# Inverses of sums in slices, two transfers and a sum moved, and one product earlier at a hand-over between two stages

## The chip, the cores and the metric

One core of one Trainium2 chip. The metric is the device time of one execution in microseconds (us), the median of several runs.

## The reference

Four sequences of 2,048 tokens with 256 channels go through pre-norm attention with 16 heads of 16 channels and then a gated feed-forward step with a shift by one token:

```
...
    logits = jnp.einsum('bhnd,bhmd->bhnm', q, k) * INV_SCALE
    attn = jax.nn.softmax(logits, axis=-1)
    h = jnp.einsum('bhnm,bhmd->bhnd', attn, v)
    concat_h = h.transpose(0, 2, 1, 3).reshape(B, N, C)
    return concat_h @ Wo.T + bo
...
        xr = mu_r * x + (1.0 - mu_r) * x_prev
        xk = mu_k * x + (1.0 - mu_k) * x_prev
        r = jax.nn.sigmoid(jnp.einsum('btc,dc->btd', xr, W_r))
        k = jnp.einsum('btc,dc->btd', xk, W_k)
        k_act = jnp.square(jax.nn.relu(k))
        out = r * jnp.einsum('btc,dc->btd', k_act, W_v)
...
x = x + attention(layernorm(x))
x = x + ffn(layernorm(x))
```

The last two lines are shortened from the reference's own.

## The kernel before

Every engine has its program written out by hand, in two stages that run into each other, and waits by semaphores. A `Steps` object is a semaphore with named steps per block: `done` counts one on, `wait(engine, block, name)` waits for it.

**The first stage** (`stage_attend`) projects q, k and v for 16 blocks of 512 tokens and then does attention in 64 rounds (`ITS`; `it` is the round, `pit` the round whose maxima are taken). A round is one group of four heads by 512 queries against 2,048 keys. It has two periods of eight steps each (`SPAN`; 128 `PERIODS`). The softmax needs each query's maximum score first. So the main loop runs two things beside each other, three periods (`LEAD`) apart: TensorE computes score tiles only to take their maxima (`peaks`, L1193), VectorE reduces each (`maxima`, L999, and L994 with ScalarE's copies), 14 packs of two reductions a period. Behind that TensorE computes the scores again, transposed (`scores`, L1137), ScalarE takes their exponentials (L922), and TensorE multiplies these with v (`times_v`, L1234). v has a column of ones, so the product holds the sum of the exponentials too. Three PSUM banks serve the maxima in turn. ScalarE copies a round's output (`keep_output`, L936) and SyncE stores it to `sums` (L706).

**What comes in ahead.** `MixInputs` prepares the second stage while the first runs. `load_constants` and `load_sums` fetch the weights and the sums of exponentials of three sequences. `invert` is VectorE's reciprocal of them (L287), 256 elements in each of 128 partitions for a sequence. `store_inverse` writes it to memory and `load_heads` reads it back spread over channels, with the numerators. GpSimd multiplies both (`heads`, L317) and adds the output bias to x (`add_to_x`, L326). VectorE's `spread_bias` and `shares_left` (L333, L352) are small preparations. All of it is placed by round on SyncE (`if it == ITS - 6`) and by period on VectorE (`first_pack(PERIODS - 6)`).

**The hand-over.** In the last three periods no maxima are left, so VectorE and the maxima's banks (5 to 7) are free. `early(k)`, k from 0 to 23, puts work of the second stage between TensorE's steps: products with Wo (`project`, L443) for blocks 0 to 3 and the turns of blocks 0 and 1 (`turn`, L453). VectorE takes each result as it comes: `residual` (L363, and statistics L367), `first_normalised` (L422), then `first_turned`, which copies a turned block out of PSUM (L431) and multiplies by the shares mu_k and mu_r (L435), and `shift` (L413), which adds the previous token's part. `free_ahead` makes TensorE wait for the bank that it writes next. The sums of x and bias of blocks 2 and 3 need x of these blocks. SyncE loads it only when the residual of two blocks before has read the buffer (`load_x`).

**The second stage** (`stage_mix`) goes over the 16 blocks in pairs. For each: product with Wk (`key`, L1649), with Wr (`receptance`, L1623), square of the rectified k (ScalarE), product with Wv (`value`, L1623), the gate times that (`gated`, L1583), and in between the residual, statistics, turn and shift of later blocks. `receptance(0)` writes banks 4 and 5, and bank 4 is where attention's output accumulates. So it waits for `s_oe`, ScalarE's copy of the last round.

The line numbers here and in the rows are those of the kernel before.

Of the kernel before, what the change touches and what calls it, by code (L numbers as in the profile page):

```python
# [21 lines left out]
P = 128  # L22
B, N, C, H = 4, 2048, 256, 16
D = C // H
KH = C // P
# [176 lines left out]
class MixInputs:  # L202
# [9 lines left out]

    EARLY, FREE = 2, 3

    def __init__(self, ctx, nc, x, sums_d, rden_d, bv, woT, bo, wrT, wkT, wvT, mu_r, mu_k):
# [68 lines left out]

    def invert(self, dve, seq):
        dve.wait_ge(self.s_den[seq], DMA)
        dve.reciprocal(self.inv[:, seq, :], self.den[:, seq, :]).then_inc(self.s_inv, 1)  # L287

    def store_inverse(self, sp, seq):
        sp.wait_ge(self.s_inv, seq + 1)  # L290
        sp.dma_start(self.rden_d[seq].rearrange("h (a w) -> (h a) w", w=self.W), self.inv[:, seq, :]
                     ).then_inc(self.s_rden[seq], DMA)
# [181 lines left out]
def stage_attend(ctx, nc, psum, x, wqT, wkT, wvT, bq, bk, q_d, k_d, kd_d, v_d, sums_d, inputs, ahead):  # L474
# [28 lines left out]
    FILLS_AHEAD = 4  # L503
    TURN_AT = 7
    FIRST_LEAD = QB + 2
    LEADS = [4] + [5] * 8 + [4]
# [164 lines left out]
    def sync(sp):  # L671
# [41 lines left out]
        def body(it):  # L713
            sp.wait_ge(s_st, unit(it * CH, 0) + 1)
            sp.wait_ge(s_vc, (it // QB) * CH + CH)
            now = range(pieces(it - 1), pieces(it))
            for n in now:
                inputs.load_k(sp, n)
            for n in now:
                inputs.load_kd(sp, n)  # L720
            for n in now:
                inputs.load_v(sp, n)
            if it + QRING - 1 < ITS:
                inputs.load_q(sp, it + QRING - 1)
            if it + 1 < ITS:
                rows(it + 1)
            sp.wait_ge(s_k, K_INC * pieces(it))
            sp.wait_ge(s_kd, K_INC * pieces(it))
            sp.wait_ge(s_v, V_INC * pieces(it))
            sp.wait_ge(s_q, Q_INC * min(it + QRING, ITS))  # L730
            out(it)
# [35 lines left out]
        for it in range(ITS):  # L767
            if it == ITS - 6:
                ahead.load_constants(sp)
                for seq in range(B - 1):  # L770
                    ahead.load_sums(sp, seq)
# [7 lines left out]
            if it == ITS - 3:  # L779
                for n in range(2, 4):  # L780
                    ahead.load_heads(sp, n)
            if it == ITS - 1:
                ahead.load_x(sp, 2)
                for seq in range(1, B - 1):
                    ahead.store_inverse(sp, seq)
                ahead.load_x(sp, 3)
                sp.wait_ge(ahead.s_rden[1], DMA)
                for n in range(4, 6):
                    ahead.load_heads(sp, n)
                for n in range(4, 6):  # L790
                    ahead.load_x(sp, n)
            body(it)

    def gpsimd(pool):
# [70 lines left out]
        for n in range(4):  # L865
            if n >= 2:
                ahead.heads(pool, n)
            ahead.add_to_x(pool, n)

# [103 lines left out]
    def vector(dve):  # L973
# [132 lines left out]
        for n in range(FULL * LEAD, PACKS):  # L1106
            if n == first_pack(PERIODS - 6):
                ahead.spread_bias(dve)
                ahead.shares_left(dve)
                ahead.invert(dve, 0)  # L1110
            maxima(n)
        of_block(ITS - 1)
        ahead.add_bias(dve, psum[:, ahead.bank_ahead(2), 0:C])
        for seq in range(1, B - 1):
            ahead.invert(dve, seq)
        for blk in range(2):
# [13 lines left out]

    def tensor(te):
        def scores(it, c, pair):
# [266 lines left out]
        for n in range(SPAN * (PERIODS - LEAD), STEPS):  # L1399
            last_fills(n, 1, n + 1, 0)  # L1400
            early(n - SPAN * (PERIODS - LEAD))
            last_fills(n + 1, 0, n + 1, 1)
            times_v(n)

# [3 lines left out]
def stage_mix(ctx, nc, psum, inputs, out):  # L1408
# [165 lines left out]
    def vector(dve):  # L1574
# [24 lines left out]
        for blk in range(0, BLOCKS, 2):  # L1599
# [3 lines left out]
            if blk == 0:  # L1603
                inputs.invert(dve, B - 1)
            if blk + 2 < BLOCKS:
# [10 lines left out]
            if blk + 4 < BLOCKS:  # L1616
                inputs.means(dve, blk // 2 + 2)
                inputs.newton(dve, blk // 2 + 2)

    def tensor(te):  # L1620
# [17 lines left out]

        def key(blk):
            vb.wait(te, blk, f"mk{KH - 1}")  # L1640
            if blk == 0:
                dx.wait(te, 2 * EARLY - 1, "x11")
            elif blk < LAST - 1:
                vy.wait(te, blk - 1, "gated")
            else:
                at.wait(te, blk, "xT1")
            for h in range(KH):
                for k in range(KH):
                    mm = te.matmul(psum[:, key_at(blk) + h, :], w_sb["k"][:, k, h * P:(h + 1) * P],  # L1649
                                   mixed["mk"][blk % 2][:, k, :], start=(k == 0), stop=(k == KH - 1))  # L1650
            pk.done(mm)

        def receptance(blk):
# [17 lines left out]

        for steps in (pk, pr, pv):
            steps.start(te)
        for blk in range(0, BLOCKS, 2):
            more = blk + 4 < BLOCKS
            key(blk)
            receptance(blk)
            if blk + 1 == LAST:
                key(blk + 1)
            value(blk)  # L1680
            receptance(blk + 1)
            if blk + 1 < LAST:
                key(blk + 1)
                turned(blk + 2)
# [8 lines left out]

    return sync, gpsimd, scalar, vector, tensor


def build(nc, a):
# [7 lines left out]
    with ExitStack() as ctx:  # L1705
# [29 lines left out]
        @block.tensor  # L1735
        def _(te):
            first[4](te)
            last[4](te)
# [23 lines left out]
```

## Time and profile before

| | |
|---|---|
| median of 3 runs | 2800.03 us (2799.42 to 2801.36) |
| the profiled execution | 2800.92 us, of which the span from first to last instruction is 2799.1 |
| busy: TensorE (PE) | 2742.8 us, 98% of the span |
| VectorE (DVE) | 2496.4 us, 89% |
| ScalarE (ACT) | 2492.9 us, 89% |
| GpSimd (POOL) | 372.9 us, 13% |
| chain that ended last | 78% TensorE, 10% SyncE's queue, 5% ScalarE, 3% VectorE |

In the attention loop three engines are near full together. Matmuls overlap in TensorE's pipeline and their ends are modelled, so its 98% does not mean that it could take in nothing more. The time is then read from who waits for whom, stage by stage. Times are in us from the start of the span.

### The profile page before, as it was taken

The page shows a single profiled execution, that of the slowest core. Times are in us where ns is not written, and L with a number is a line of the kernel's source. Part 1 is how long each engine was busy: PE and PEld are TensorE (multiplying, and loading weights), DVE is VectorE, ACT ScalarE, POOL GpSimd, SP SyncE. Part 2 cuts the span into 40 slices and gives each one's busy share as a digit, 9 for nine tenths or more (in the row PEclk, how much of TensorE's full clock was granted, in tenths as well). Part 3 has the DMA queues.
Part 4 walks back from the last instruction along what each step waited for, and adds up shares of the span by engine and source line. Part 5 has one row for each costly group of instructions (what it writes and reads, how often), then busy time and mean ns, then how long its engine had stood idle before and what let it go on. Part 6 is the DMA issues. An engine that isn't in the chain of part 4 may idle for free.

```text
span 2799.1 us, 59961 instructions
## 1 busy us (share of the span) xinstructions
PE 2742.8 (98%) x23628; PEld 924.0 (33%) x23628; DVE 2496.4 (89%) x4797; ACT 2492.9 (89%) x2874; POOL 372.9 (13%) x751
## 2 busy tenths in 40 slices
PE   8999999999999999999999999999999999999999
PEld 4543222222222222222222222222222222224776
DVE  4567999999999999999999999999999999985774
ACT  6767999999999999999999999999999999996555
POOL 6762000000000000000000000000000000113451
PEclk9999999999999999999999999999999999999999
DMA  4642000000000000101010101010100001212431
GB/s 161 206 152 79 22 22 22 22 22 22 22 22 22 20 24 15 29 9 31 11 33 11 33 11 33 11 33 11 31 13 27 17 20 42 58 36 87 157 129 46
DMA packets 135288, 124.34 MB, mean 44 GB/s; under 512 B 49888, under 2 KB 117344, under 8 KB 135008
## 3 DMA queue, kind: packets, MB, share of 16 engines
q1 hardware_dynamic: 135008, 120.52, 14.0%
q8 instruction: 187, 3.06, 0.4%
q14 instruction: 93, 0.76, 0.1%
HBM read 72.75 MB, written 47.19 MB: 43 GB/s over the span
## 4 chain that ended last, share of the span: by engine, by line
PE 78%; SPq 10%; ACT 5%; DVE 3%; issue 2%; DMA 2%; ACTq 0%; DVEq 0%
PE psum L1234 33%; PE psum L1137 17%; PE psum L1193 15%; SPq L153 3%; PE psum L1257 3%; PE psum L1623 2%; SPq L158 2%; PE psum L1152 2%; PE psum L443 2%; SPq L126 2%; SPq L127 2%; DMA a_qs<-q_parts 2%; PE psum L1268 2%; PE psum L1649 2%; ACT m_gate L922 1%
## 5 line engine op out<-in xcount | busy, mean ns | idle before, releaser
L999 DVE TENSOR_REDUCE a_mx<-psum 128x1 f32<-128x512 f32 x3096 | 1948.6, 685 | 121.3 <-PE psum L1193 100.5
L1137 PE MATMUL psum<-a_qs,a_ks 50*128 50x512 f16 x4096 | 793.2, 384 | 11.8 <-ACT m_gate L922 1.2
L922 ACT ACTIVATE m_gate<-psum 128x1024 f32<-128x1024 f32 x684 | 674.5, 1034 | 41.2 <-PE psum L1137 38.3
L922 ACT ACTIVATE p_x<-psum 128x1024 f32<-128x1024 f32 x682 | 672.7, 1034 | 41.6 <-PE psum L1137 39.0
L1193 PE MATMUL psum<-a_ks,a_qs 48*128 48x512 f16 x3596 | 696.2, 383 | 13.7 <-DVE a_mx L999 5.5
L922 ACT ACTIVATE m_y<-psum 128x1024 f32<-128x1024 f32 x682 | 672.7, 1034 | 38.6 <-PE psum L1137 35.8
L1234 PE MATMUL psum<-m_gate,a_vst 128*32 128x256 f32 (+1 forms) x4568 | 414.8, 435 | 1.6 <-ACT m_gate L922 0.9
L1234 PE MATMUL psum<-p_x,a_vst 128*32 128x256 f32 (+1 forms) x4568 | 412.4, 433 | 0.8
L1234 PE MATMUL psum<-m_y,a_vst 128*32 128x256 f32 (+1 forms) x4552 | 411.8, 433 | 0.8
L1137 PEld LDWEIGHTS psum<-a_qs,a_ks 50*128 50x128 f16 x4096 | 199.1, 93 | 610.1 <-ACT m_gate L922 135.2
L994 DVE CUSTOM_DVE_ANT_0 a_copied<-psum,a_copied 128x512 f32<-128x512 f32 x500 | 323.6, 685 | 23.6 <-PE psum L1193 23.6
L1193 PEld LDWEIGHTS psum<-a_ks,a_qs 48*128 48x128 f16 x3596 | 175.0, 93 | 463.6 <-DVE a_mx L999 368.3
L931 ACT ACTIVATE a_copied<-psum 128x1024 f32<-128x1024 f32 x250 | 260.6, 1042 | 0.1
L808 POOL MEMSET a_mx<- 128x8 f32 x64 | 7.2, 112 | 1384.9 <-DVE a_m L978 1384.9
L801 POOL COPY a_vst<-a_vin 128x64 f32<-128x64 f32 x256 | 59.7, 236 | 754.4 <-PE psum L1234 754.4
L1234 PEld LDWEIGHTS psum<-m_gate,a_vst 128*32 128x32 f32 x4568 | 90.5, 108 | 191.5 <-issue 174.7
L1234 PEld LDWEIGHTS psum<-p_x,a_vst 128*32 128x32 f32 x4568 | 90.6, 108 | 189.9 <-issue 175.1
L1234 PEld LDWEIGHTS psum<-m_y,a_vst 128*32 128x32 f32 x4552 | 90.2, 108 | 190.0 <-issue 174.7
L1152 PE MATMUL psum<-a_kd,a_qs 48*128 48x512 f16 x500 | 97.2, 381 | 0.0
L823 POOL TENSOR_TENSOR m_split<-m_whole,m_split 128x512 f16<-128x512 f32 x64 | 73.6, 1156 | 74.1 <-ACT m_split L910 73.7
L908 ACT ACTIVATE m_whole<-psum,p_sb,p_gain 128x512 f32<-128x512 f32 x64 | 49.4, 772 | 28.9 <-PE psum L1257 28.8
L363 DVE TENSOR_TENSOR m_whole<-psum,m_x 128x512 f32<-128x512 f32 x24 | 16.5, 690 | 56.6 <-PE psum L443 56.6
(126 smaller groups left out, 1636.9 us busy)
## 6 DMA issues: line engine op xcount, KB each, us to landing
m_x<-x SPq DMA_DIRECT2D x24, 512.0 KB, 5.8
a_qs<-q_parts SPq DMA_DIRECT2D x384, 32.0 KB, 2.1
sums<-a_o SPq DMA_DIRECT2D x256, 34.0 KB
q_parts<-m_split SPq DMA_DIRECT2D x16, 512.0 KB, 3.2
v_rows<-m_v SPq DMA_DIRECT2D x16, 512.0 KB, 2.7
k_parts<-m_split SPq DMA_DIRECT2D x16, 512.0 KB, 3.9
a_ks<-k_parts SPq DMA_DIRECT2D x64, 128.0 KB
a_vin<-v_rows SPq DMA_DIRECT2D x64, 128.0 KB, 5.5
```

Source lines behind the costliest of these rows:

```text
L153: sp.dma_start(self.qs[row:row + D, it % QRING, :].rearrange("p (u t) -> p u t", u=GP), src[a, par]).then_inc(self.s_q, DMA)
L801: pool.tensor_copy(v_st[:, c, :, 0:D], v_in[:, u % 2, c, :].rearrange("p (g d) -> p g d", g=G)).then_inc(s_vc, 1)
L823: least.done(pool.tensor_tensor(parts[s][:, j, 1, :], full[s][:, j, :], parts[s][:, j, 0, :], ALU.subtract))
L922: ac.activation(p_sb[n % WEIGHTS][:, 2 * pair:2 * pair + 2, :], psum[:, at:at + 2, :], ACT.Exp, scale=SCALE).then_inc(s_exp, 1)
L931: ac.activation(copied[:, :, :], psum[:, at:at + 2, :], ACT.Relu).then_inc(s_exp, 1)
L994: dve.tensor_tensor_reduce(out=copied[:, par, :], in0=psum[:, bank(at), :], in1=copied[:, par, :], scale=1.0, scalar=LEAST, op0=ALU.add, o ...
L999: dve.tensor_reduce(peak, psum[:, bank(at), :], AX.X, ALU.max).then_inc(s_mx, 1)
L1137: mm = te.matmul(psum[:, pair_of_banks(u) + par, :], ks[row:row + MR, (it // QB) % 2, pair, c * P:(c + 1) * P], qs[row:row + MR, it % QRIN ...
L1152: mm = te.matmul(psum[:, pair_of_banks(u) + par, :], qs[row:row + SR, pit % QRING, at:at + P], kd[row:row + SR, (pit // QB) % 2, pair, :], ...
L1193: te.matmul(psum[:, bank(slot(n, par)), :], qs[row:row + SR, pit % QRING, at:at + P], keys, start=True, stop=True).then_inc(s_sp, 1)
L1234: mm = te.matmul(psum[32 * g:32 * g + 32, O, at:at + width], v_st[:, c, g, :], p_sb[n % WEIGHTS][:, g, at:at + width], start=(c == 0), sto ...
L1257: mm = te.matmul(psum[:, j % 2, :], w_sb[n][:, k, h * P:(h + 1) * P], xnT[blk % 2][:, k, :], start=(k == 0), stop=(k == KH - 1))
```

## The change

Four edits:

1. `invert` becomes eight slices of 32 elements (`SLICES`). Those of sequences 0 to 2 (24 slices) are put one in every five packs (`APART`) of the maxima, from sixteen periods before the end on. The copies of `spread_bias` and the `shares_left` go to the starts of the eighteenth and the seventeenth period before the end. Before, both and the inverse of sequence 0 stood in one place six periods before the end, and the inverses of sequences 1 and 2 stood after the last maximum. Sequence 3's inverse, in the second stage, is cut into eight slices in its place. The loads of weights and sums move from round `ITS - 6` to `ITS - 11`.
2. On SyncE the load of x of block 2 goes into the round before last, behind the rows of maxima, and the stores of the inverses of sequences 1 and 2 go to round `ITS - 3`. Both stood at the start of the last round.
3. GpSimd's sum for block 3 waits for VectorE's last share of block 1 (`mr1`).
4. TensorE's product with Wk of block 0 is issued ahead of the last product with v.

```
-    def invert(self, dve, seq):
-        dve.wait_ge(self.s_den[seq], DMA)
-        dve.reciprocal(self.inv[:, seq, :], self.den[:, seq, :]).then_inc(self.s_inv, 1)
+    def invert(self, dve, seq, n):
+
+        if n == 0:
+            dve.wait_ge(self.s_den[seq], DMA)
+        at = bass.ds(n * (self.W // self.SLICES), self.W // self.SLICES)
+        dve.reciprocal(self.inv[:, seq, at], self.den[:, seq, at]).then_inc(self.s_inv, 1)
...
+            if it == ITS - 2:
+                ahead.load_x(sp, 2)
...
-            if it == ITS - 6:
+            if it == ITS - 11:
                 ahead.load_constants(sp)
...
             if it == ITS - 3:
                 for n in range(2, 4):
                     ahead.load_heads(sp, n)
-            if it == ITS - 1:
-                ahead.load_x(sp, 2)
                 for seq in range(1, B - 1):
                     ahead.store_inverse(sp, seq)
+            if it == ITS - 1:
                 ahead.load_x(sp, 3)
...
+            if n == 3:
+                ahead.at.wait(pool, 1, f"mr{KH - 1}")
             ahead.add_to_x(pool, n)
...
-            if n == first_pack(PERIODS - 6):
+            if n == first_pack(PERIODS - 18):
                 ahead.spread_bias(dve)
+            if n == first_pack(PERIODS - 17):
                 ahead.shares_left(dve)
-                ahead.invert(dve, 0)
+            piece, left = divmod(n - first_pack(PERIODS - 16), APART)
+            if left == 0 and 0 <= piece < (B - 1) * ahead.SLICES:
+                ahead.invert(dve, piece // ahead.SLICES, piece % ahead.SLICES)
             maxima(n)
         of_block(ITS - 1)
         ahead.add_bias(dve, psum[:, ahead.bank_ahead(2), 0:C])
-        for seq in range(1, B - 1):
-            ahead.invert(dve, seq)
...
+            if n == STEPS - 1:
+                beside_last(te)
             times_v(n)
...
-                inputs.invert(dve, B - 1)
+                for n in range(inputs.SLICES):
+                    inputs.invert(dve, B - 1, n)
...
+    def first_key(te):
+
+        pk.start(te)
+        key(te, 0)
```

`beside_last` is `first_key` of the second stage. `key` moved out of that stage's TensorE program unchanged, which no longer calls it for block 0.

On VectorE, at the sixth period before the end (`a_mx` the maxima, `m_inv` the inverses, `m_den` the sums), the kernel before has:

```order
L994 ISA a_mx 128x1
L333 COPY m_bvs<-m_bv 128x128 x2
L352 TENSOR_SCALAR m_restmk<-m_mk 128x2
L352 TENSOR_SCALAR m_restmr<-m_mr 128x2
L287 RECIPROCAL m_inv<-m_den 128x256
L999 TENSOR_REDUCE a_mx<-psum 128x1
```

Nothing stands between the maxima there now. Ten periods earlier the changed kernel has this, where the one before has reductions alone:

```order
L291 RECIPROCAL m_inv<-m_den 128x32
L1007 TENSOR_REDUCE a_mx<-psum 128x1
L986 TENSOR_REDUCE a_m<-a_mx 128x16
L1007 TENSOR_REDUCE a_mx<-psum 128x1 x5
L1002 ISA a_copied,a_mx<-psum,a_copied 128x512
L1002 ISA a_mx 128x1
L1002 ISA a_copied,a_mx<-psum,a_copied 128x512
L1002 ISA a_mx 128x1
L1007 TENSOR_REDUCE a_mx<-psum 128x1 x2
L291 RECIPROCAL m_inv<-m_den 128x32
L1007 TENSOR_REDUCE a_mx<-psum 128x1 x10
L291 RECIPROCAL m_inv<-m_den 128x32
```

Ten reductions, five packs, lie from slice to slice.

On SyncE's queue over the last rounds (`a_mrows` the rows of maxima, `sums` a round's store) the kernel before has:

```order
L699 DMA a_qs<-a_mrows 1x8x128 x4
L706 DMA sums<-a_o 17x512 x4
L699 DMA a_qs<-a_mrows 1x8x128 x4
L706 DMA sums<-a_o 17x512 x4
L308 DMA m_x<-x 128x4x256
L291 DMA inverse_denominators<-m_inv 128x256 x2
L308 DMA m_x<-x 128x4x256
L301 DMA m_num<-sums 128x1x512
```

and the changed one:

```order
L295 DMA inverse_denominators<-m_inv 128x256 x2
L704 DMA a_qs<-a_mrows 1x8x128 x4
L711 DMA sums<-a_o 17x512 x4
L704 DMA a_qs<-a_mrows 1x8x128 x4
L312 DMA m_x<-x 128x4x256
L711 DMA sums<-a_o 17x512 x4
L312 DMA m_x<-x 128x4x256
L305 DMA m_num<-sums 128x1x512
```

The two stores of inverses moved ahead of two rounds, and the first load of x ahead of one store of sums.

On TensorE, where the first stage ends (L1234 is v, L1649 Wk, L1623 Wr and Wv), before:

```order
L1137 MATMUL psum<-a_qs,a_ks 128x512 x4
L1234 MATMUL psum<-p_x,a_vst 32x512 x4
L1234 MATMUL psum<-m_gate,a_vst 32x512 x4
L1649 MATMUL psum<-m_split,m_wk 128x512 x4
L1623 MATMUL psum<-m_wr,m_split 128x256 x8
```

and in the changed kernel:

```order
L1146 MATMUL psum<-a_qs,a_ks 128x512 x4
L1243 MATMUL psum<-p_x,a_vst 32x512 x4
L1642 MATMUL psum<-m_split,m_wk 128x512 x4
L1243 MATMUL psum<-m_gate,a_vst 32x512 x4
L1654 MATMUL psum<-m_wr,m_split 128x256 x8
```

The product with Wk stands between the last two with v now, and Wr's follows the last with v directly.

## Rows read from the trace of the kernel before

**Rows 1.** Timeline, SyncE's queue, stores of sums: start, length, engine, line, operation, count.

```profile
1834.14 1.27 SPq L706 DMA_DIRECT2D sums<-a_o  x4
1870.28 1.27 SPq L706 DMA_DIRECT2D sums<-a_o  x4
1906.71 1.28 SPq L706 DMA_DIRECT2D sums<-a_o  x4
...
2377.09 1.28 SPq L706 DMA_DIRECT2D sums<-a_o  x4
...
2416.53 1.27 SPq L706 DMA_DIRECT2D sums<-a_o  x4
```

**Rows 2.** Timeline, VectorE, six periods before the end of the maxima.

```profile
2392.25 0.36 DVE L333 COPY m_bvs<-m_bv 128x128 f32<-128x128 f32 x2
...
2392.59 0.16 DVE L352 TENSOR_SCALAR m_restmr<-m_mr 128x2 f32<-128x2 f32 x1
2392.66 1.75 DVE L287 RECIPROCAL m_inv<-m_den 128x256 f32<-128x256 f32 x1
2394.32 0.63 DVE L999 TENSOR_REDUCE a_mx<-psum 128x1 f32<-128x512 f32 x1
```

**Rows 3.** Windows: length, busy (count) of PE, PEld, DVE, ACT, POOL, granted clock, DMA.

```profile
2395.00:2398.60 3.60, 3.59 (x16) 0.58 (x16) 2.14 (x5) 0.64 (x1) 0.94 (x5) 0.53 0.00 0
...
2548.80:2552.20 3.40, 3.40 (x11) 1.47 (x14) 3.37 (x8) 0.75 (x1) 0.00 (x0) 0.50 0.43 163
```

**Rows 4.** Timeline, VectorE, an ordinary period; brackets hold the wait before a row.

```profile
2306.21 0.69 DVE L994 CUSTOM_DVE_ANT_0 a_copied<-psum,a_copied 128x512 f32<-128x512 f32 x1 [0.36 <-PE psum L1193]
...
2307.44 11.31 DVE L999 TENSOR_REDUCE a_mx<-psum 128x1 f32<-128x512 f32 x18
```

**Rows 5.** Waits over the whole span: us in total, times, longest.

```profile
PEld psum L1193 <- DVE a_mx L999: 368.3, 895, 1.9
```

**Rows 6.** Timeline, TensorE at the hand-over, products with Wo.

```profile
2541.01 1.13 PE L443 MATMUL psum<-m_wo,m_hT 128*128 128x256 f32 x4
...
2543.71 1.13 PE L443 MATMUL psum<-m_wo,m_hT 128*128 128x256 f32 x4
...
2548.80 2.07 PE L443 MATMUL psum<-m_wo,m_hT 128*128 128x256 f32 x4 [2.31 <-DVE m_xT L431]
...
2553.07 1.13 PE L443 MATMUL psum<-m_wo,m_hT 128*128 128x256 f32 x4
```

**Rows 7.** Timeline, VectorE at the hand-over, shares of mu and a residual.

```profile
2537.98 3.45 DVE L435 TENSOR_SCALAR m_split<-m_xT,m_mk 128x512 f32<-128x512 f32 x2
2541.35 3.99 DVE L435 TENSOR_SCALAR m_split<-m_xT,m_mr 128x512 f32<-128x512 f32 x2
...
2549.25 0.88 DVE L435 TENSOR_SCALAR m_split<-m_xT,m_mk 128x512 f32<-128x512 f32 x2
...
2553.69 1.28 DVE L363 TENSOR_TENSOR m_whole<-psum,m_x 128x512 f32<-128x512 f32 x2
```

**Rows 8.** Timelines of GpSimd, SyncE's queue and VectorE at the hand-over.

```profile
2537.36 2.36 POOL L326 TENSOR_TENSOR m_x<-m_x,m_bo 128x1024 f32<-128x1024 f32 x1 [17.01 <-DMA m_x<-x]
...
2542.52 2.54 POOL L326 TENSOR_TENSOR m_x<-m_x,m_bo 128x1024 f32<-128x1024 f32 x1
...
2529.14 0.40 SPq L308 DMA_DIRECT2D m_x<-x  x1
...
2517.72 0.69 DVE L363 TENSOR_TENSOR m_whole<-psum,m_x 128x512 f32<-128x512 f32 x1 [4.64 <-PE psum L443]
```

**Rows 9.** Timelines of TensorE and ScalarE where the first stage ends.

```profile
2568.73 1.07 PE L1234 MATMUL psum<-m_gate,a_vst 128*32 128x512 f32 x8 [0.88 <-ACT m_gate L922]
...
2573.27 1.03 PE L1623 MATMUL psum<-m_wr,m_split 128*128 128x256 f32 x4
...
2569.87 0.58 ACT L936 COPY a_o<-psum 128x512 f32<-128x512 f32 x1 [1.19 <-PE psum L1234]
```

**Rows 10.** Timeline, VectorE, first pair of the second stage.

```profile
2597.96 1.22 DVE L1583 TENSOR_TENSOR m_y<-psum,m_gate 128x1024 f32<-128x1024 f32 x1
```

More of the change, by code:

```diff
@@ L213 @@
     EARLY, FREE = 2, 3
+    SLICES = 8
     def __init__(self, ctx, nc, x, sums_d, rden_d, bv, woT, bo, wrT, wkT, wvT, mu_r, mu_k):
@@ L283, in load_sums @@
                      ).then_inc(self.s_den[seq], DMA)
-    def invert(self, dve, seq):
-        dve.wait_ge(self.s_den[seq], DMA)
-        dve.reciprocal(self.inv[:, seq, :], self.den[:, seq, :]).then_inc(self.s_inv, 1)
+    def invert(self, dve, seq, n):
[3 more added lines that the diff above has]
+        dve.reciprocal(self.inv[:, seq, at], self.den[:, seq, at]).then_inc(self.s_inv, 1)
     def store_inverse(self, sp, seq):
-        sp.wait_ge(self.s_inv, seq + 1)
+        sp.wait_ge(self.s_inv, (seq + 1) * self.SLICES)
         sp.dma_start(self.rden_d[seq].rearrange("h (a w) -> (h a) w", w=self.W), self.inv[:, seq, :]
@@ L504, in stage_attend @@
     TURN_AT = 7
+    APART = 5
     FIRST_LEAD = QB + 2
@@ L1129, in vector, with tensor @@
         ahead.newton(dve, 1)
-    def tensor(te):
+    def tensor(te, beside_last):
         def scores(it, c, pair):
@@ L1618, in vector, with key @@
                 inputs.newton(dve, blk // 2 + 2)
+    def key(te, blk):
+        vb.wait(te, blk, f"mk{KH - 1}")
+        if blk == 0:
+            dx.wait(te, 2 * EARLY - 1, "x11")
+        elif blk < LAST - 1:
+            vy.wait(te, blk - 1, "gated")
+        else:
+            at.wait(te, blk, "xT1")
+        for h in range(KH):
+            for k in range(KH):
+                mm = te.matmul(psum[:, key_at(blk) + h, :], w_sb["k"][:, k, h * P:(h + 1) * P],
+                               mixed["mk"][blk % 2][:, k, :], start=(k == 0), stop=(k == KH - 1))
+        pk.done(mm)
+    def first_key(te):
+        pk.start(te)
+        key(te, 0)
     def tensor(te):
@@ L1637, in turned @@
             inputs.turn(te, blk, [psum[:, turned_at(blk) + h, :] for h in range(KH)])
[L1639 to L1651, printed above, removed]
         def receptance(blk):
@@ L1670, in value @@
                     pv.done(mm)
-        for steps in (pk, pr, pv):
+        for steps in (pr, pv):
             steps.start(te)
@@ L1675, in tensor @@
             more = blk + 4 < BLOCKS
-            key(blk)
+            if blk:
+                key(te, blk)
             receptance(blk)
             if blk + 1 == LAST:
-                key(blk + 1)
+                key(te, blk + 1)
             value(blk)
@@ L1682, in tensor @@
             if blk + 1 < LAST:
-                key(blk + 1)
+                key(te, blk + 1)
                 turned(blk + 2)
@@ L1692, in tensor @@
                 proj(blk + 5)
-    return sync, gpsimd, scalar, vector, tensor
+    return sync, gpsimd, scalar, vector, tensor, first_key
 def build(nc, a):
@@ L1736, in _ @@
         def _(te):
-            first[4](te)
+            first[4](te, last[5])
             last[4](te)
```

## The prediction

> **What bounds the kernel now.** I read the page first, then the issue times of the stores of sums for the rhythm of the attention loop, then the timeline of VectorE and the list of waits for what sets that rhythm, and last the timelines of all engines over the hand-over to the second stage. The change touches only the last fifth of the run.
>
> The stores of sums mark one round (`it`, two periods) each. An ordinary round takes 36.14 us (1834.14 to 1870.28). Two others are longer: 36.43 us (to 1906.71), and 39.44 us (2377.09 to 2416.53) [rows 1]. The reader is to see two things. The 0.29 us of the first is not made good later, so the loop has no play over a round. And the long round holds the present inverse of sequence 0: VectorE does two copies, two small operations and the whole reciprocal in one piece, from 2392.25 to the next reduction at 2394.32, 2.07 us [rows 2]. It cost 39.44 - 36.14 = 3.30 us. That is more than its length because TensorE, left without a free bank, fell to a granted clock of 0.53 over the next 3.60 us (mostly the 1.2 GHz level), though it was busy for 3.59 of them [rows 3].
>
> In an ordinary period no engine has much room. VectorE waits 0.36 us for scores ahead of one piece, and then runs 18 reductions in 11.31 us [rows 4]. In the other direction TensorE's weight loads for the scores of the maxima (L1193) wait for a reduction 895 times [rows 5]. There are 1,798 packs of maxima, so in half of them TensorE stands ready for VectorE.
>
> At the hand-over TensorE goes on in steps of 2.70 us (products with Wo at 2541.01 and 2543.71), then stands 2.31 us for VectorE's copy of the second block's turned x and restarts at half clock: the next two such products begin at 2548.80 and 2553.07. From 2543.71 to 2553.07 are 9.36 us where two steps are 5.40, a loss of 3.96 us [rows 6]; the granted clock is 0.50 from 2548.80 to 2552.20 [rows 3]. VectorE is late because its shares of mu (L435) take 3.45 and 3.99 us a pair, where the same pair takes 0.88 later [rows 7]. GpSimd is in its sums to x and its product of heads then, from 2537.36 to 2545.06, and it is there so late because it waited 17.01 us for x of block 2, whose load was issued at 2529.14 [rows 8].
>
> **The change part by part.** Loads of weights and sums five rounds sooner: the same issues on SyncE's queue, eight loads and three of sums, ahead of a round's loads of k and v that the loop needs a round and more later. Cost nothing, as long as that lead lasts.
>
> The lump goes: -3.30 us, with the half clock behind it.
>
> The copies and shares left are made alone, 2.07 - 1.66 = 0.41 us of VectorE, and 24 slices of 32 elements come into the loop. The whole reciprocal holds VectorE 1.66 us (2392.66 to 2394.32), an operation on two elements 0.07 (2392.59 to 2392.66) [rows 2], so (1.66 - 0.07) / 254 = 0.0063 us an element and a slice 0.07 + 30 x 0.0063 = 0.26 us; 24 of them are 6.2 us. The lowest that a slice can be is an eighth of 1.66, 0.21 us (5.0 us in all). The highest is the recorded duration of the small operation, 0.16, plus 0.19: 0.35 us (8.4 us in all). What they do to the end is the unknown of this change. Below stands 0: one slice falls in every five packs, some three a period, 0.74 us, and VectorE's waits of a period (0.36 us, and a share of the 11.31) could swallow most of it. Above stands all of it, since the 0.29 us of [rows 1] was kept whole. I take a half, the share of packs in which TensorE already waits for VectorE [rows 5]: 3.1 us, and 0.2 us for the copies. A slice costs where the next weight load waits for the reduction behind it, and nothing where VectorE would have waited. One slice is an eighth of the wait that lowered the clock, so I charge no clock.
>
> The Trainium skill ("VectorE: DVE Perf Modes", the section on the TRN2 errata) says that operations read from SBUF pay a fixed extra latency each, some 150 cycles in all by its measurement. By that page's figure, an estimate, a slice would be 0.16 us of fixed time and 0.20 of work, and a half of 24 such slices 4.3 us instead of 3.1. The trace sides with 0.07: the next operation starts before the former's recorded end.
>
> The whole inverses of sequences 1 and 2 leave the tail. There VectorE waits for products with Wo, 4.64 us ahead of the row at 2517.72 [rows 8], so this gives nothing. Their stores and block 2's load leave the end of SyncE's queue. The load then waits only for the residual of block 0 (2517.72 + 0.69 = 2518.4) instead of 2529.14. By the 8.2 us from that issue to GpSimd's start, x is there at about 2526.6, so the sum of block 2 (2.36) and the product of heads of block 3 (2.8, between the two sums of [rows 8]) end by about 2531.8, before VectorE's shares begin at 2537.98. On SyncE's queue only the next round's store of sums stands behind this load, and it waits for later work anyway.
>
> The sum of block 3 is held until the last share of block 1. So both pairs of block 0 run alone: 3.45 + 3.99 - 2 x 0.88 gives about 5.7 us back, and the copy that released TensorE at 2548.80 comes by about 2543.1, ahead of 2546.4, when TensorE asks. The stall goes: -3.96 us.
>
> First product with Wk ahead of the last with v: TensorE now waits 0.88 us for the last exponential, before 2568.73 [rows 9]. The product with Wk fills that from 2567.85 on. But behind it come the last product with v, ScalarE's copy of the output and only then the product with Wr, which uses the output's bank; in the present order Wk's product covers that copy. From 2568.73 to 2573.27 are 4.54 us, some 1.00 of them v's product and 3.54 Wk's. New: 2567.85 + 3.54 (Wk) + 1.14 (v, to the start of the copy) + 0.58 (copy) = 2573.1, with the hand-over about 2573.2, against 2573.27 now [rows 9]. I count -0.1 us; the whole 0.88 would need the bank to be free.
>
> Sequence 3's inverse in eight slices: 8 x 0.26 - 1.66 = +0.44 us, in front of the gating operation at 2597.96, which shows no wait before it and releases TensorE's next product with Wk [rows 10]. I let it count in full.
>
> Sum: -3.30 + 3.1 + 0.2 - 3.96 - 0.1 + 0.44 = -3.6 us. On the profiled execution's own 2800.92 that is 2797.3; that one lies 0.9 above the median of the runs, so I forecast 2796.4.
>
> **The rivals.** *Slices free.* If VectorE's waits take up slices and copies, the sum is -6.9 us: 2793.1. For it: 0.36 us of one wait is more than a slice. Against it: 0.29 us kept whole, and half of TensorE's loads waiting for VectorE. With all 0.88 of the Wk product too it would be -7.7 us, 2792.3.
>
> *Slices dearer than their length, slower than before.* The lump cost 3.30 for 2.07, 1.6 for one. Should each slice stop TensorE, ScalarE behind it, and cost by that factor, 24 x 0.26 x 1.6 = 10.0 us: the sum is +3.3 us, 2803.3. It decides from 0.28 us a slice on. Against it: the surplus of the lump came with the half clock.
>
> *The stall only moves.* The held sum runs beside VectorE's shift of block 1. By the Trainium skill ("SBUF — State Buffer", "SBUF: two separate sides") the port that the two engines share is locked by whoever comes first, for VectorE's operations with two SBUF inputs too, which the shift's are. From rows: the shares of block 1 end at about 2550.9 now (two pairs from 2549.25 [rows 7]), so 5.7 us sooner at 2545.2; the first half of block 2's residual is out at about 2554.3 now [rows 7], 3.4 us later; with the sum's 2.54 in between it would be out at 2551.1. TensorE needs its bank four steps after 2546.4, at 2557.2. The play is 6.1 us, so this decides only beyond that. If x of block 2 came late all the same, the 3.96 would stay: 2800.4.
>
> **How the numbers follow.** Slices that cost between a fifth and full length: 0.60, the likeliest, 2796.4. Slices free: 0.20, about 2793. Slices dearer than their length: 0.10, 2800 to 2803.3. Stall kept or moved: 0.10, about 2800. The range reaches from 2792.8, the free case, to 2799.8, slices at full 6.2 us (-0.3 us). A measurement tells about 0.2%, 5.6 us, from no change. Only the free case passes it below (under 2794.4), with a little of the first: 0.21. Above it only slices at twice their length would come: 0.03. The rest is 0.76.
>
> **What would show it.** Round lengths from the stores of sums: the 39.44 gone, and over the eight or nine periods with slices rounds of about 36.9 instead of 36.14 (36.2 if free, 37.6 if in full). No granted clock below 1 near 2395. VectorE's shares at 0.9 a pair, GpSimd's sum of block 2 before them, Wo's products at 2.70 without a gap and no half clock there. A wait of some 0.8 us ahead of the first product with Wr. Wrong would be: a new gap of TensorE in the last 24 steps, slices over 0.3 us apart, or a later loss in the second stage, where GpSimd and VectorE meet again.

## The result, and the profile after

The changed kernel takes 2794.82 us in the median of 22 runs (2793.74 to 2797.22), the one before 2799.27 us in the median of 22 (2797.23 to 2802.48). The ratio is 0.9985, with a 95% interval of 0.9978 to 0.9991, and the medians lie 4.45 us apart. The forecast was 2796.4 us, 3.6 us below the 2800.03 of the three runs known then. The profiled execution of the changed kernel has a span of 2793.7 us, against 2799.1 before.

The page of the changed kernel: the span, part 1 (busy time, share and count by engine) and one group of part 5, the weight loads for the scores of the maxima.

```profile
span 2793.7 us, 59990 instructions
PE 2740.2 (98%) x23628; PEld 923.1 (33%) x23628; DVE 2492.0 (89%) x4825; ACT 2496.0 (89%) x2874; POOL 374.8 (13%) x751
...
L1202 PEld LDWEIGHTS psum<-a_ks,a_qs 48*128 48x128 f16 x3596 | 174.8, 93 | 465.2 <-DVE a_mx L1007 369.2
```

The page says almost nothing of the change. The wait of the weight loads for VectorE is what it was (369.2 us against 368.3 [rows 5]). The difference has to be read by stage, so the two traces are cut at the same four instructions. Each length is a difference of two start times.

| stretch | before | after | difference | forecast |
|---|---|---|---|---|
| the last 20 periods with maxima (starts of VectorE's groups of copying maxima) | 365.03 | 363.18 | -1.85 | 0.0 |
| product of the bias to the first product with Wr | 67.71 | 63.77 | -3.94 | -4.06 |
| first product with Wr to block 2's product with Wk | 26.06 | 26.22 | +0.16 | +0.44 |
| first product with Wr to the end | 225.80 | 225.92 | +0.12 | |

The first two and the last (which holds the third) make -5.67 us of the -5.4 between the spans. The rest is drift in stretches that no edit touches. Over all kernels measured below, the last stretch lies between 225.1 and 226.8 us, and it differs by 0.7 us between the kernel before and only_transfers, which have the same second stage. All that runs ahead of the 20 periods takes between 2135.8 and 2138.2 us. A term of one or two microseconds can therefore not be read from a single execution, only from its own stretch. The stretches themselves repeat well: the five kernels with the slices in the changed kernel's places have 363.05 to 363.18 us for the 20 periods, the two with the lump 364.92 and 365.03.

**The loop.** SyncE's stores of sums in the changed kernel, as in [rows 1]:

```profile
2196.54 1.27 SPq L711 DMA_DIRECT2D sums<-a_o  x4
2232.92 1.25 SPq L711 DMA_DIRECT2D sums<-a_o  x4
2269.41 1.28 SPq L711 DMA_DIRECT2D sums<-a_o  x4
2305.92 1.28 SPq L711 DMA_DIRECT2D sums<-a_o  x4
2342.28 1.27 SPq L711 DMA_DIRECT2D sums<-a_o  x4
2378.81 1.28 SPq L711 DMA_DIRECT2D sums<-a_o  x4
2414.98 1.27 SPq L711 DMA_DIRECT2D sums<-a_o  x4
```

The round of 39.44 us is gone. The five rounds with slices take 36.38, 36.49, 36.51, 36.36 and 36.53 us, not the 36.9 of the forecast, and the last, without them, 36.17.

**The hand-over.** Timeline of TensorE in the changed kernel, products with Wo, as in [rows 6]:

```profile
2539.50 1.13 PE L447 MATMUL psum<-m_wo,m_hT 128*128 128x256 f32 x4
...
2542.20 1.13 PE L447 MATMUL psum<-m_wo,m_hT 128*128 128x256 f32 x4
...
2544.90 1.13 PE L447 MATMUL psum<-m_wo,m_hT 128*128 128x256 f32 x4
```

Steps of 2.70 us throughout and no wait. The view of windows (columns as in [rows 3]) gives a granted clock of 1.00 where it was 0.50:

```profile
2545.00:2552.00 7.00, 7.00 (x42) 2.88 (x46) 6.21 (x10) 5.34 (x6) 3.68 (x3) 1.00 0.13 38
```

The timelines of VectorE and GpSimd there, as in [rows 7] and [rows 8]:

```profile
2536.47 0.87 DVE L439 TENSOR_SCALAR m_split<-m_xT,m_mk 128x512 f32<-128x512 f32 x2
2537.25 0.88 DVE L439 TENSOR_SCALAR m_split<-m_xT,m_mr 128x512 f32<-128x512 f32 x2
...
2538.19 1.41 DVE L417 SCALAR_TENSOR_TENSOR m_split<-m_xT,m_restmk,m_split 128x512 f32<-128x512 f32 x2
...
2540.85 1.28 DVE L435 COPY m_xT<-psum 128x512 f32<-128x512 f32 x2
...
2543.83 3.54 DVE L417 SCALAR_TENSOR_TENSOR m_split<-m_xT,m_restmk,m_split 128x512 f32<-128x512 f32 x2
...
2548.62 1.28 DVE L367 TENSOR_TENSOR m_whole<-psum,m_x 128x512 f32<-128x512 f32 x2
```

```profile
2521.05 2.37 POOL L330 TENSOR_TENSOR m_x<-m_x,m_bo 128x1024 f32<-128x1024 f32 x1 [2.23 <-DMA m_x<-x]
...
2543.79 2.37 POOL L330 TENSOR_TENSOR m_x<-m_x,m_bo 128x1024 f32<-128x1024 f32 x1 [14.16 <-DVE m_split L439]
```

GpSimd's sum of block 2 is done 13 us before VectorE's shares, which run at 0.87 and 0.88 us a pair. The copy that TensorE waited for starts at 2540.85 and ends at 2542.13, 2.8 us before TensorE's next product with Wo at 2544.90. The stall did move, as the third rival had it: the held sum meets VectorE's shift at 2543.8, whose first pair takes 3.54 us instead of 1.41. But those 2.13 us fall into a play of several: VectorE takes the next residual from 2548.62 on, and TensorE goes on without a gap. The Trainium skill ("SBUF — State Buffer", "SBUF: two separate sides") says that VectorE's operations with two SBUF inputs and GpSimd's share a port, and that whoever starts first has it for the whole instruction while the other is blocked. The trace agrees: GpSimd's sum runs from 2543.79 to 2546.16, and VectorE's pair, begun at 2543.83, is done at 2547.37, only 1.21 us behind it.

### The profile page after: what moved, and what is told of

Same layout as the page of the kernel before. It is cut to its first block, busy times and chain, and to the rows that moved or that the text cites. A ratio compares the mean times of both kernels' runs of the same rounds, so it can differ in the third digit from the quotient of the medians.

```text
span 2793.7 us, 59990 instructions
## 1 busy us (share of the span) xinstructions
PE 2740.2 (98%) x23628; PEld 923.1 (33%) x23628; DVE 2492.0 (89%) x4825; ACT 2496.0 (89%) x2874; POOL 374.8 (13%) x751
## 4 chain that ended last, share of the span: by engine, by line
PE 79%; SPq 9%; ACT 4%; DVE 3%; issue 2%; DMA 2%; ACTq 0%
PE psum L1243 33%; PE psum L1146 17%; PE psum L1202 15%; PE psum L1266 3%; SPq L153 3%; PE psum L1654 2%; SPq L158 2%; PE psum L1161 2%; PE psum L447 2%; SPq L126 2%; SPq L127 2%; DMA a_qs<-q_parts 2%; PE psum L1277 2%; PE psum L1642 2%; ACT m_gate L930 1%
## 5 line engine op out<-in xcount | busy, mean ns | idle before, releaser
L1202 PEld LDWEIGHTS psum<-a_ks,a_qs 48*128 48x128 f16 x3596 | 174.8, 93 | 465.2 <-DVE a_mx L1007 369.2
```

What stands on the lines that cost most here:

```text
L1202: te.matmul(psum[:, bank(slot(n, par)), :], qs[row:row + SR, pit % QRING, at:at + P], keys, start=True, stop=True).then_inc(s_sp, 1)
```

## The experiments

Each kernel below was timed in turn with the kernel before. "Loop" is the length of the last 20 periods with maxima (before 365.03, after 363.18), "hand-over" that from the bias's product to the first with Wr (before 67.71, after 63.77).

**Only the transfers and the held sum (only_transfers).** The kernel before with a part of edit 2, block 2's load of x in the round before last, and with edit 3, the hold. All inverses whole and in their old places, the product with Wk too.

```
+            if it == ITS - 2:
+                ahead.load_x(sp, 2)
             ...
-                ahead.load_x(sp, 2)
             ...
+            if n == 3:
+                ahead.at.wait(pool, 1, f"mr{KH - 1}")
```

> The kernel before with two parts of the change alone: block 2's load of x in the round before last, and GpSimd's sum for block 3 held until the last share of block 1. The inverses stay where they were, in one piece each. My theory (the terms add): the lump of 2.07 us and the half clock behind it stay, so the longest round stays at 39.4 us; TensorE's wait of 2.31 us and the half clock at the hand-over go, and from the bias product to the first product with Wr it takes 63.8 us instead of 67.7. In all 3.9 us less than before. Rival (the two are tied: without slices VectorE is late at the hand-over for the whole inverses of sequences 1 and 2): part of the wait stays, 1 to 3 us less than before.

Measured: median 2795.56 us, ratio 0.9985 (0.9975 to 0.9994). Loop 364.92, hand-over 63.75. All of the hand-over's gain is here, and none of the loop's. Neither the inverses in the tail nor the order around Wk have a part in it.

**The hold taken out (no_hold).** The changed kernel without edit 3.

```
-            if n == 3:
-                ahead.at.wait(pool, 1, f"mr{KH - 1}")
```

> The changed kernel without the wait of GpSimd's sum for block 3. My theory: x of block 3 is issued at 2527.7 and there by 2533.3 to 2536, so the sum (2.4 us) meets the statistics' last steps, the normalisation or the shares of block 0. VectorE loses up to 2.4 us there; in the changed kernel its copy for TensorE begins at 2540.85 and TensorE asks at 2544.9, so there are 2.9 us of play and the hand-over stays at 63.8 us: the same time as the changed kernel within 0.3 us. Rival (the hold is what removes the stall): the wait comes back with the half clock, 2 to 4 us more than the changed kernel.

Measured: median 2795.04, ratio 0.9984 (0.9975 to 0.9993), hand-over 63.76. The timelines of GpSimd, VectorE and TensorE in this kernel:

```profile
2535.50 2.52 POOL L330 TENSOR_TENSOR m_x<-m_x,m_bo 128x1024 f32<-128x1024 f32 x1 [7.02 <-DMA m_x<-x]
...
2535.31 2.99 DVE L439 TENSOR_SCALAR m_split<-m_xT,m_mk 128x512 f32<-128x512 f32 x2
...
2541.81 1.28 DVE L435 COPY m_xT<-psum 128x512 f32<-128x512 f32 x2
...
2543.74 1.13 PE L447 MATMUL psum<-m_wo,m_hT 128*128 128x256 f32 x4
```

Without the hold the sum of block 3 does fall on one pair of shares, which takes 2.99 us. The copy then begins at 2541.81, later, but still before TensorE needs the bank. The hold gives 2 us of play and no time.

**The load late, the hold kept (late_load).** The changed kernel with the load of block 2 back at the start of the last round.

```
-            if it == ITS - 2:
-                ahead.load_x(sp, 2)
             ...
             if it == ITS - 1:
+                ahead.load_x(sp, 2)
                 ahead.load_x(sp, 3)
```

> The changed kernel with block 2's load of x at the start of the last round again, the held sum kept. It asks which of the two edits takes the stall away; without the hold the stall stayed away. My theory: x of block 2 is issued at 2527.7 and its sum runs from about 2535.5, the product of heads behind it to about 2540.7; both meet VectorE's shares and shift of block 0, which lose some 4 us; the copy for TensorE then comes at about 2546 against 2544.9. A wait of some 1.3 us comes back, too short for the half clock: 65.1 us from the bias product to the first with Wr in place of 63.8. Rival 1 (the hold alone is enough): 63.8. Rival 2 (the whole stall with the half clock): 67.7.

Measured: median 2795.23, ratio 0.9983 (0.9974 to 0.9992), hand-over 64.42, where 65.1 was expected. The timelines of GpSimd, VectorE and TensorE:

```profile
2534.61 2.36 POOL L330 TENSOR_TENSOR m_x<-m_x,m_bo 128x1024 f32<-128x1024 f32 x1 [17.40 <-DMA m_x<-x]
...
2534.85 3.82 DVE L439 TENSOR_SCALAR m_split<-m_xT,m_mk 128x512 f32<-128x512 f32 x2
2538.59 1.89 DVE L439 TENSOR_SCALAR m_split<-m_xT,m_mr 128x512 f32<-128x512 f32 x2
...
2543.93 1.13 PE L447 MATMUL psum<-m_wo,m_hT 128*128 128x256 f32 x4 [0.59 <-DVE m_xT L435]
```

The sum of block 2 and the heads behind it still meet both pairs, but the second for a part only, so TensorE stands 0.59 us, with no half clock behind it. In the changed kernel either of the two edits without the other therefore removes most of the 3.94 us: the early load all of it, the hold all but 0.65. Neither was tried alone on the kernel before, where two whole inverses and their stores still stand in the tail, so what the hold gives there is not shown. Only with both of GpSimd's sums and the heads between them in one row, as before, did TensorE stand 2.31 us.

**The slices taken out (no_slices).** The changed kernel without the 24 slices. The inverses of sequences 0 to 2 are not computed (ones stand in their place, written ahead of the loop).

```
+        dve.memset(ahead.inv[:, 0:B - 1, :], 1.0).then_inc(ahead.s_inv, (B - 1) * ahead.SLICES)
         ...
-            if left == 0 and 0 <= piece < (B - 1) * ahead.SLICES:
-                ahead.invert(dve, piece // ahead.SLICES, piece % ahead.SLICES)
```

> The changed kernel with the 24 slices left out of the maxima. The inverses of sequences 0 to 2 are ones, written once ahead of the loop, so the division by the sums is left out for these sequences; loads, stores and all else are the same. It measures what the slices cost. My theory after the result: slices and copies together cost 1.8 us in the loop, the slices nearly all of it, so the loop is 1.6 us shorter (1.3 to 1.8) than in the changed kernel. Rival 1 (slices hide in VectorE's waits and the remainder comes from the loads of weights five rounds sooner and the copies): less than 0.4 us. Rival 2 (half of their length of 0.26 us, the prediction): 3.1 us.

Measured: median 2794.17, ratio 0.9977 (0.9968 to 0.9987), loop 361.74. Two terms come apart here. 365.03 - 361.74 = 3.29 us is the lump with its half clock, net of the copies and shares in their new place. The round in which these stand takes 36.23 us in no_slices (stores at 2158.83 and 2195.06) and 36.15 before (2159.97 and 2196.12), so they cost 0.08 at most. And 363.18 - 361.74 = 1.44 us is the price of the 24 slices, 0.06 us each.

**The slices at VectorE's waits (slices_at_waits), and away from them (slices_elsewhere).** Same slices, same count, same sixteen periods; only the packs before which they stand differ. `place` gives a pack's period and its number there.

```
-    APART = 5
+    SLOTS = ((0, 2), (0, 5), (1, 2), (1, 3), (1, 5))
...
+            period, k = place(n)
+            if period >= PERIODS - 16 and (period % 2, k) in SLOTS:
+                piece = (period - PERIODS + 16) // 2 * len(SLOTS) + SLOTS.index((period % 2, k))
...
slices_elsewhere:
+    SLOTS = ((0, 7), (0, 10), (1, 7), (1, 10), (1, 13))
```

> The changed kernel with the same 24 slices in five places of a round: ahead of the packs 2, 3 and 5 of one period and 2 and 5 of the other, where VectorE waits for scores in the trace of before (0.44 and 0.33 us ahead of 3 and 2, 0.28 ahead of the other 2, some 0.1 ahead of 5). Measured against the kernel without slices, whose last 20 periods take 361.74 us; in the changed kernel they take 363.18, so that its slices cost 1.44. My theory (a slice costs what is left of it after VectorE's own wait): ahead of 2, 3 and 2 nothing, ahead of the two 5 some 0.1 each: 10 x 0.1 = 1 us at most, 362.0 to 362.7 us. Rival (the place does not matter, each slice costs 0.06 us): 363.2.

> As the run before, with the places of a round ahead of the packs 7 and 10 of one period and 7, 10 and 13 of the other, where VectorE goes from reduction to reduction with no wait and TensorE's next weight load waits for it. My theory: each slice costs nearly its length, 24 x 0.15 to 0.21 us, 365.3 to 366.8 us for the last 20 periods (361.74 without slices). Rival (place does not matter): 363.2.

Measured: at the waits median 2793.50, ratio 0.9978 (0.9968 to 0.9987), loop 361.75, that is 0.01 us for 24 slices, or nothing within the 0.1 us by which this stretch repeats, and below the 362.0 to 362.7 expected. Elsewhere 2798.14, ratio 0.9995 (0.9986 to 1.0005), loop 366.26, that is 4.52 us, 0.19 a slice, as expected. Timeline of VectorE from a pair of copying maxima to the next, first without slices:

```profile
2213.14 1.29 DVE L1007 TENSOR_REDUCE a_mx<-psum 128x1 f32<-128x512 f32 x2 [0.22 <-PE psum L1201]
...
2215.64 11.43 DVE L1007 TENSOR_REDUCE a_mx<-psum 128x1 f32<-128x512 f32 x18
2226.99 0.68 DVE L1002 CUSTOM_DVE_ANT_0 a_copied<-psum,a_copied 128x512 f32<-128x512 f32 x1
```

with them at the waits:

```profile
2213.36 0.34 DVE L291 RECIPROCAL m_inv<-m_den 128x32 f32<-128x32 f32 x1
2213.66 1.29 DVE L1007 TENSOR_REDUCE a_mx<-psum 128x1 f32<-128x512 f32 x2
...
2216.16 1.29 DVE L1007 TENSOR_REDUCE a_mx<-psum 128x1 f32<-128x512 f32 x2
2217.36 0.34 DVE L291 RECIPROCAL m_inv<-m_den 128x32 f32<-128x32 f32 x1
2217.62 9.96 DVE L1007 TENSOR_REDUCE a_mx<-psum 128x1 f32<-128x512 f32 x16
2227.50 0.68 DVE L1002 CUSTOM_DVE_ANT_0 a_copied<-psum,a_copied 128x512 f32<-128x512 f32 x1
```

and elsewhere:

```profile
2217.18 4.00 DVE L1007 TENSOR_REDUCE a_mx<-psum 128x1 f32<-128x512 f32 x6
2221.10 0.34 DVE L291 RECIPROCAL m_inv<-m_den 128x32 f32<-128x32 f32 x1
2221.36 3.72 DVE L1007 TENSOR_REDUCE a_mx<-psum 128x1 f32<-128x512 f32 x6
2225.00 0.34 DVE L291 RECIPROCAL m_inv<-m_den 128x32 f32<-128x32 f32 x1
...
2228.90 0.68 DVE L1002 CUSTOM_DVE_ANT_0 a_copied<-psum,a_copied 128x512 f32<-128x512 f32 x1
```

A slice holds VectorE for 0.26 us (2221.10 to 2221.36) in either. The first stands in the 0.22 us that VectorE waited for scores anyway. The second stands early in the streak of 18 reductions, whose 11.35 us can hold short waits that the view doesn't list: an average of 0.63 us a reduction, where two that nothing holds up take 0.60 each (2216.16 to 2217.36). With that slice in the streak it still ends as before (2215.64 to 2226.99 is 11.35, 2216.16 to 2227.50 is 11.34). Later in the streak (2217.18 to 2228.90 is 11.72) two slices cost 0.37. There the first six reductions take 3.92 us (2217.18 to 2221.10), the next six 3.64 (2221.36 to 2225.00), so the short waits lie early in the streak and VectorE has hardly any left behind them.

**Larger pieces at the same places (quarters_at_waits).** `SLICES = 4` with slices_at_waits' places: 12 pieces of 64 elements.

> The kernel with slices at VectorE's waits, with 12 slices of 64 elements (about 0.42 us each) in place of 24 of 32 (0.21). It asks how large a piece those waits hold. My theory (a slice costs what is left after VectorE's own wait, and after TensorE's slack at the next load): ahead of 3 nothing, ahead of the two 2 some 0.1, ahead of the two 5 some 0.2 to 0.3; 12 slices 1.5 to 2 us, 363.2 to 363.8 us for the last 20 periods. Rival (the waits are play of the whole loop and hold the same total in any pieces): 361.8.

Measured: median 2794.36, ratio 0.9981 (0.9972 to 0.9990), loop 363.01: 1.27 us over no_slices. Some 0.3 of it is not theirs: one round behind the last piece takes 36.44 us (stores at 2414.34 and 2450.78), where the changed kernel has 36.17. The 12 pieces so cost about 1.0 us, under the 1.5 to 2 of the theory, but not the rival's 0. A piece of twice the size no longer fits wholly into the same places.

**Whole inverses in the loop (whole_in_loop).** The changed kernel with `SLICES = 1` and `APART = 40`, three whole reciprocals in different rounds (sequence 3's whole too).

> The changed kernel with the three inverses whole in the loop, 40 packs apart from the sixteenth period before the end on, in place of 24 slices. Each holds VectorE 1.66 us. The lump before had 2.07 us and cost 3.29. My theory: TensorE stands some 1.2 to 1.4 us each time, shorter than the 1.64 us behind which the clock fell; if the clock holds, each costs 1.3 to 1.6 us and the last 20 periods take 365.6 to 366.6 us. Rival (a stop of that length is enough for the half clock of 3.4 us): 2.9 us each, 370.4 us, and three stretches of half clock.

Measured: median 2799.83, ratio 1.0005 (0.9995 to 1.0014), loop 368.98: 7.24 us for three, 1.4, 2.9 and 2.8 by the rounds of stores. That lies between the two forecasts, 366.6 at most if the clock held and 370.4 if it fell each time: it held once and fell twice. TensorE stops for each. Its timeline, the only waits over 0.2 us around each, and windows behind the first two:

```profile
2211.75 0.39 PE L1202 MATMUL psum<-a_ks,a_qs 48*128 48x512 f16 x2 [1.14 <-DVE a_mx L1007]
...
2264.76 0.39 PE L1202 MATMUL psum<-a_ks,a_qs 48*128 48x512 f16 x2 [1.37 <-DVE a_mx L1007]
...
2319.65 0.39 PE L1202 MATMUL psum<-a_ks,a_qs 48*128 48x512 f16 x2 [1.50 <-DVE a_mx L1007]
```

```profile
2214.00:2218.00 4.00, 4.00 (x45) 1.15 (x37) 3.94 (x9) 3.65 (x6) 0.00 (x0) 1.00 0.00 0
...
2266.70:2270.10 3.40, 3.40 (x22) 0.54 (x20) 2.30 (x4) 2.05 (x2) 0.24 (x1) 0.57 0.00 0
```

The stop of 1.14 us left the clock at 1.00 and cost 1.4 us. Those of 1.37 and 1.50 us were each followed by 3.4 us near the 1.2 GHz level and cost twice that, of which 0.2 to 0.4 us is the longer stop itself. So cutting the inverses matters for two reasons: a piece's own length, and that no stop comes near those behind which the clock fell.

**The product with Wk back (key_behind), and other banks for the first Wr (other_banks).** The first puts it behind the last product with v again. The second keeps it in front and lets `receptance(0)` write banks 0 and 1, so that it waits for no copy of the output; block 1's waits for that copy instead.

```
key_behind:
+            times_v(n)
             if n == STEPS - 1:
                 beside_last(te)
-            times_v(n)
other_banks:
-        return KEY if blk == LAST else REC
+        return {0: OUT, LAST: KEY}.get(blk, REC)
...
-            if blk == 0:
+            if blk == 1:
                 te.wait_ge(inputs.s_oe, ITS)
```

> The changed kernel with the first product with Wk behind the last product with v again, as before. My theory: the wait of 0.80 us ahead of the product with Wr goes and a wait of 0.88 us ahead of the last product with v comes back; the distance from the last product but one with v to the first with Wr stays 6.5 us within 0.1. No difference in the whole. Rival (the edit is worth the wait it fills): 0.8 us more than the changed kernel.

> The changed kernel with block 0's product with Wr written to banks 0 and 1, which the scores have left, in place of 4 and 5; the wait for ScalarE's copy of the last output moves to block 1's. The wait of 0.80 us ahead of Wr goes. My theory (the product with Wk ahead of the last with v gains nothing only because of the bank): the distance from the bias product to the first with Wr falls from 63.8 to 63.0 us and the whole by 0.8. Rival (ScalarE, which squares only behind that copy, or VectorE takes it back): the distance falls, and the first stretch up to block 2's product with Wk is longer by as much.

Measured: key_behind 2794.99, ratio 0.9982 (0.9972 to 0.9991), hand-over 63.75: the same as after. other_banks 2794.79, ratio 0.9983 (0.9974 to 0.9993), hand-over 62.90, 0.87 us shorter. Timeline of TensorE in the changed kernel:

```profile
2562.31 3.70 PE L1642 MATMUL psum<-m_split,m_wk 128*128 128x512 f32 x8
2565.94 1.06 PE L1243 MATMUL psum<-m_gate,a_vst 128*32 128x512 f32 x8
2567.80 3.69 PE L1654 MATMUL psum<-m_wr,m_split 128*128 128x256 f32 x16 [0.80 <-ACT a_o L944]
```

and in other_banks:

```profile
2565.32 1.07 PE L1243 MATMUL psum<-m_gate,a_vst 128*32 128x512 f32 x8
2566.32 3.72 PE L1654 MATMUL psum<-m_wr,m_split 128*128 128x256 f32 x16
```

The wait for the exponential became a wait for ScalarE's copy, 0.88 against 0.80 us. With the bank free the gap is gone. In the median nothing of it shows against after (2794.79 and 2794.82). The stretch from the first Wr to the end is 226.56 us there against 225.92, but it is 226.5 in no_hold and key_behind too, so whether the 0.87 us is given back or lies under the drift is open.

**All that helped (combined).** slices_at_waits, other_banks, and sequence 3's inverse in one piece.

```
-                for n in range(inputs.SLICES):
-                    inputs.invert(dve, B - 1, n)
+                dve.wait_ge(inputs.s_den[B - 1], DMA)
+                dve.reciprocal(inputs.inv[:, B - 1, :], inputs.den[:, B - 1, :]).then_inc(inputs.s_inv, inputs.SLICES)
```

> What the runs so far point to: the changed kernel with the slices at VectorE's waits, block 0's product with Wr in banks 0 and 1, and sequence 3's inverse whole again in its place in the second stage. If the terms add: 361.75 us for the last 20 periods (changed kernel 363.18), 62.9 from the bias product to the first with Wr (63.8), and 0.1 to 0.2 less up to block 2's product with Wk. In all 2.4 us less than the changed kernel, a median near 2792.4. Rival (the second stage, which differs by up to 1.5 us from kernel to kernel so far, takes a part back): 2793 to 2794.

Measured: median 2793.13 us, ratio 0.9975 (0.9966 to 0.9984), the lowest of all, though its interval overlaps that of slices_at_waits, and 2792.4 were expected. Loop 361.87, hand-over 62.90, and then block 2's product with Wk comes 26.65 us behind the first with Wr instead of 26.22. Against the changed kernel these stretches make -1.31 - 0.87 + 0.43 = -1.75 us, where -2.4 was expected. Timelines of VectorE, GpSimd and TensorE:

```profile
2585.76 1.74 DVE L1618 RECIPROCAL m_inv<-m_den 128x256 f32<-128x256 f32 x1
2587.41 0.60 DVE L412 COPY m_xT<-m_xT 128x2 f32<-128x2 f32 x1
...
2585.49 2.50 POOL L321 TENSOR_TENSOR m_hT<-m_num,m_rden 128x512 f32<-128x512 f32 x2 [9.21 <-DMA m_rden<-inverse_denominators]
...
2592.07 3.67 PE L1644 MATMUL psum<-m_split,m_wk 128*128 128x512 f32 x8 [0.48 <-DVE m_y L1596]
```

VectorE's copy of two elements takes 0.60 us instead of 0.10 in after, beside GpSimd's product of heads, and stands in the chain that releases TensorE. So 0.43 us of the gain goes to this meeting. The earlier hand-over alone does not bring it about: in other_banks, with the same 62.90, GpSimd's heads end at 2588.13, just before the copy at 2588.40, and the stretch is 26.24. Counted from the first product with Wr, the heads begin 0.8 us later in combined than there, behind a load of inverses that, so counted, SyncE also issued 0.8 us later. Why it did is open.

## Why the prediction was right, and where it was not

**The lump, -3.30 us: right.** no_slices against before gives -3.29. By whole_in_loop a little under half of such a cost is the clock: 1.4 us without the half clock, 2.8 and 2.9 with it, behind stops that were 0.2 to 0.4 us longer.

**The hand-over's stall, -3.96 us: right**, -3.94 in the stretch, with each step of its chain seen: x early, sum before the shares, shares at 0.88 us a pair, copy in time, no half clock. What the prediction had too strong is the part of each edit: it let the hold and the early load together free VectorE's shares, but in the changed kernel the early load is enough without the hold (63.76 us against 63.77), and the hold without the early load nearly so (64.42).

**The slices, +3.1 us: mis-sized, 1.44.** The length was right (0.26 us in the loop). Wrong was "a half, the share of packs in which TensorE already waits for VectorE". The same 24 slices cost 0.01 or 4.52 us by their places, so no share of packs prices them; what does is whether VectorE has a wait in that stretch of the period. Five and 14 have no common divisor, so one in five packs walks over all places of a period, and the price of 1.44 us lies between the two, at 23% of the full 6.2 us. The second rival (slices above their length, 0.28 us or more) is excluded, even at the worst places tried (0.19).

**The copies and shares, +0.2: 0.08 at most**, by the one round of no_slices that holds them.

**Sequence 3 in slices, +0.44 (8 x 0.26 - 1.66 is 0.42): mis-sized, 0.16 at most.** The kernel key_behind, with the second stage's products in the order of before, has 26.14 us in this stretch against 26.06, and the changed order has 26.22 with slices and 26.13 with the inverse whole (whole_in_loop): 0.08 or 0.09 for the slices. Timeline of VectorE in the changed kernel:

```profile
2588.12 1.81 DVE L291 RECIPROCAL m_inv<-m_den 128x32 f32<-128x32 f32 x8
2589.86 0.10 DVE L412 COPY m_xT<-m_xT 128x2 f32<-128x2 f32 x1
```

From the first slice to the next operation are 1.74 us, 0.22 each, against 1.66 for the whole one [rows 2]. The 0.07 us read from a two-element operation is not a part of each slice's length; the lowest bound, an eighth of 1.66, was nearly right. In the loop, with a reduction from PSUM behind it, 0.26 us pass. Why is not shown.

**The product with Wk, -0.1: none**, as argued: the wait moves to the copy of the output. That the bank was the reason is shown by other_banks.

The terms with their measured sizes are -3.29 + 1.44 - 3.94 + 0.16 = -5.6 us, against -5.4 between the spans and -4.45 between the medians. The medians differ by 0.9 us less because the profiled execution before lay 1.65 us above its kernel's median here (2800.92 against 2799.27) and that of the changed kernel 0.76 above its own (2795.58 against 2794.82).

Some of the agreement of the totals is luck. The sum of terms was 2.0 us off (-3.6 against -5.6), most of it by the slices, and for the reason just given the medians show only 0.9 of this (4.45 us apart, not 3.6). The median came out 1.6 us below the forecast, which is nearly as near to the "slices free" rival (about 2793) as to the forecast, so the total alone could not have told the two apart; the 1.44 us of the loop did. The range begins at 2792.8, where its own free case adds up to 2793.1. That changes nothing here.

## What to carry to other kernels

In a loop where two engines wait for each other in turn, a small operation can cost nothing where its engine would have waited anyway and most of its length elsewhere (here 0.19 of 0.26 us). List the waits by place in the period before spreading work evenly, and keep pieces so small that TensorE's stops stay below those behind which its clock fell. When two edits remove one stall, take out each alone, since the stall may need all of its causes at once. And an operation put into a gap only moves the gap, if what follows needs a buffer that the displaced work fills.

## What the hardware showed that was not expected

Stops of TensorE of 0.59, 0.80, 0.88 and 1.14 us left its granted clock at 1.00. Those of 1.37, 1.50, 1.64 (in the lump of the kernel before) and 2.31 us [rows 6] were each followed by some 3.4 us at 0.50 to 0.57, the 1.2 GHz level, although TensorE was busy all that time. A mean such as 0.57 mixes both levels at the window's edges. No run here shows whether the length of the stop alone decides.

Eight reciprocals of 32 elements back to back took 1.74 us where one of 256 takes 1.66: cutting it into eighths costs 5%.
